# One core, one attention and FP4 feed-forward layer: two accumulators change places, four steps of the hand-written engine orders are moved

## What is computed

```python
y  = layernorm(x)
y1 = LN(y  + causal_attention(y, y, y))        # gains g1, beta1
y2 = LN(y1 + attention(y1, ctx, ctx))          # gains g2, beta2
y3 = LN(y2 + relu(y2 @ w1 + b1) @ w2 + b2)     # 256 -> 1024 -> 256, gains g3, beta3
x1 = x + y3
n  = layernorm(x1)
h  = silu(q(n) @ q(w_gate).T) * (q(n) @ q(w_up).T)   # 256 -> 704
out = x1 + q(h) @ q(w_down).T                        # 704 -> 256
```

## Time and profile before

| what | value |
|---|---|
| time of the profiled execution | 672.63 us |
| its span, first to last instruction | 670.7 us |
| median of the three runs | 672.4 us |
| mean granted TensorE clock | 0.949 |
| TensorE matmul busy | 573.5 us (86%) |
| TensorE weight loads busy | 540.4 us (81%) |
| VectorE busy | 531.6 us (79%) |
| ScalarE busy | 382.1 us (57%) |
| GpSimd busy | 344.4 us (51%) |

### The profile page before, as it was taken

One profiled execution on the slowest core, in us unless ns is written; L12 is line 12 of the kernel. 1 busy time (PEld: TensorE's weight loads), 2 busy tenths in 40 slices (PEclk: granted clock), 3 DMA queues, 4 the chain that ended last, 5 costly groups with the idle time before them and its releaser, 6 DMA issues.

```text
span 670.7 us, 12397 instructions
## 1 busy us (share of the span) xinstructions
PE 573.5 (86%) x3989; PEld 540.4 (81%) x3989; DVE 531.6 (79%) x1305; ACT 382.1 (57%) x779; POOL 344.4 (51%) x444
## 2 busy tenths in 40 slices
PE   2734877999899989999999999998999999988575
PEld 1623776989898989898989889898989898888564
DVE  3965636988887988888888889898879888888763
ACT  3423536666675747475756666665748474756341
POOL 3322235656554755566555655565557555555422
PEclk9575779999999999999999999999999999999986
DMA  7330000101010101000010102010101000000000
GB/s 234 88 98 0 0 33 0 41 1 49 0 56 1 35 15 32 25 23 23 0 55 0 47 0 55 0 47 0 54 1 32 1 24 9 10 9 9 8 17 16
DMA packets 18726, 19.30 MB, mean 29 GB/s; under 512 B 1520, under 2 KB 18176, under 8 KB 18688
## 3 DMA queue, kind: packets, MB, share of 16 engines
q1 hardware_dynamic: 18688, 18.82, 9.4%
HBM read 14.62 MB, written 4.19 MB: 28 GB/s over the span
## 4 chain that ended last, share of the span: by engine, by line
PE 53%; DVE 27%; issue 8%; ACT 6%; POOL 2%; DMA 2%; SPq 1%; DVEq 0%; ACTq 0%; POOLq 0%
PE R L851 4%; PE R L853 4%; PE R L852 4%; PE O L899 3%; PE R L918 3%; PE O L966 3%; PE O L964 3%; PE O L965 3%; PE TR L766 3%; PE R L920 3%; PE R L919 3%; PE R L766 3%; DVE hs L1219 3%; DVE hqT_lo L1252 2%; DVE hT_lo L1246 2%
## 5 line engine op out<-in xcount | busy, mean ns | idle before, releaser
L437 POOL TENSOR_TENSOR rs<-mv,neg_half 128x1 f32<-128x1 f32 (+1 forms) x112 | 68.1, 614 | 43.8 <-DVE mv L1166 41.8
L851 PE MATMUL R<-gu_hi,xqT_hi 128*128 128x352 f32 x256 | 85.5, 334 | 2.3 <-ACT xqT_hi L599 1.1
L918 PE MATMUL R<-y2T_hi,w_hi 128*128 128x256 f32 x256 | 76.7, 300 | 8.0 <-DVE y2T_lo L1302 5.8
L853 PE MATMUL R<-gu_hi,xqT_lo 128*128 128x352 f32 x256 | 82.5, 322 | 0.0
L852 PE MATMUL R<-gu_lo,xqT_hi 128*128 128x352 f32 x256 | 82.5, 322 | 0.0
L443 POOL TENSOR_TENSOR hs<-hh,h_rec 128x704 f32<-128x704 f32 x32 | 44.5, 1392 | 68.5 <-DVE h_rec L1202 68.5
L635 ACT ACTIVATE hqT_hi<-R 128x768 fp32r<-128x768 f32 x32 | 26.0, 812 | 91.3 <-PE R L766 91.3
L964 PE MATMUL O<-w_hi,hT_hi 128*128 128x256 f32 x256 | 74.0, 289 | 0.0
L920 PE MATMUL R<-y2T_hi,w_lo 128*128 128x256 f32 x256 | 72.9, 285 | 0.0
L919 PE MATMUL R<-y2T_lo,w_hi 128*128 128x256 f32 x256 | 72.7, 284 | 0.0
L966 PE MATMUL O<-w_hi,hT_lo 128*128 128x256 f32 x256 | 72.6, 283 | 0.0
(11 more groups left out here) (148 smaller groups left out, 1859.2 us busy)
## 6 DMA issues: line engine op xcount, KB each, us to landing
x_in<-in_x SPq DMA_DIRECT2D x16, 256.0 KB, 2.8
x_res<-in_x SPq DMA_DIRECT2D x16, 256.0 KB, 2.8
out<-x SPq DMA_DIRECT2D x32, 128.0 KB, 1.7
hT<-in_L_xattn_w SPq DMA_DIRECT2D x2, 1024.0 KB, 7.2
ctx_rows<-in_ctx SPq DMA_DIRECT2D x16, 64.0 KB, 2.6
wd_raw<-in_L_ffn_w_down SPq DMA_DIRECT2D x1, 704.0 KB, 11.5
w_raw<-in_L_ffn_w_gate SPq DMA_DIRECT2D x1, 640.0 KB, 5.2
w_raw<-in_L_ffn_w_up SPq DMA_DIRECT2D x1, 640.0 KB, 6.8
```

Of the source, the lines that this page charges most:

```text
L437: pool.tensor_tensor(rs[i][:, t0:t0 + len(ts)], mv[i][:, t0:t0 + len(ts), 1], neg_half[:, 0:len(ts)], ALU.pow).then_inc(ln_rstd[i], 1)
L851: mm(o, xh, gu_hi[:, c, m, cols], start=(c == 0), stop=False)
L853: last = mm(o, xl, gu_hi[:, c, m, cols], start=False, stop=(c == KC - 1))
L918: mm(o, w1_hi[:, c, cols], y2T_hi[:, c, :], start=(c == 0), stop=False)
```

## The change

The same instructions are issued, with the same operands except for the accumulators; they stand in another order on four engines.

- `values` and `down` of tile t now use O[t], so tile 0's values wait for `cross_sum` and tile 1's for `ff_sum`; `ff2` of tile 0 waits for both `down_add`, `cross_values` for the first alone. The second `down_add` moves from behind the products of h to behind `x_max` of tile 1.
- VectorE: the low halves of tile 1's turned h stand ahead of x's block maximum of tile 0 (they stood behind x's reciprocal). The small second piece of `hT_lower` is a function of its own, `hT_stack`. The low half of tile 0's turned h is taken in the slot before, ahead of the second `ff_sum`, and the first two steps of a slot are now the reciprocal and the sum of the self attention. `z3_stats(1)` stands ahead of `x1_sum(0)`; `h_lower` of group 3 moves up to group 2; `cross_max` stands ahead of `h_lift(0)`; the statistics of z2 stand ahead of h's second scale.
- ScalarE: the turned y2 is copied ahead of the first layer norm (`norm_x`); `warm(Exp)` stands ahead of `abs_h(0)`; `norm(2)` stands ahead of `abs_h(1)`; `relu_upper(3)` stands ahead of the second silu.
- GpSimd: `y_rows` of z2 and `context_values` stand at the slot's start, ahead of `unscale_h(1)`; `residual` stands behind `unscale_h(0)`; `power(1)` ahead of `masks`; `power(2)` ahead of `scale_h(1)`.

SyncE's list is unchanged. In it the stores of x2 stand behind a wait for `residual`.

```diff
@@ gpsimd, slot
                 prepare(b, h, "early")
+                if f:
+                    y_rows(b, h, False, 0)
+                    y_rows(b, h, False, 1)
                 if f1:
                     gamma3(b, g, 0)
+                if live(b, h, 0) and h == 0:
...
+                    context_values(b)
                 if q1:
                     unscale_h(b, g, 1)
...
                 if q:
                     unscale_h(b, h, 0)
+                if f:
+                    residual(b, h)
+                prepare(b, h, "late")
+                if a:
+                    power(2, b, h, A, (0, 1))
+                if q:
                     scale_h(b, h, 1)
-                prepare(b, h, "late")
-                if a:
-                    power(2, b, h, A, (0, 1))
@@ scalar, slot
                 if q:
                     silu(b, h, 1, (1,))
+                    warm(b, h, ACT.Exp, 1)
                     abs_h(b, h, 0)
-                    warm(b, h, ACT.Exp, 1)
@@ tensor, values
-                    wait(pe, z3_set, b, h, F + 1, T, T)
-                else:
-                    wait(pe, z2_set, b, h, F, T, T)
+                    wait(pe, z2_set, b, h, F, T, T)
+                else:
+                    wait(pe, z3_set, b, h, F + 1, T, T)
...
-                    last = mm(O[1 - t][:, 0:D + 1], e, y0[:, key, :], start=(i == 0), stop=(i == len(lhs) - 1))
+                    last = mm(O[t][:, 0:D + 1], e, y0[:, key, :], start=(i == 0), stop=(i == len(lhs) - 1))
@@ vector, slot
                 prepare(b, h, "early")
-                if q1:
-                    hT_lower(b, g, 0)
-                if f1:
-                    shift(3, b, g, F, (0,))
                 if a:
                     self_reciprocal(b, h, 0)
                     self_sum(b, h, 0)
                 if q1:
+                    hT_stack(b, g, 0)
+                if f1:
+                    shift(3, b, g, F, (0,))
...
                 if f1:
+                    z3_stats(b, g, 1)
                     x1_sum(b, g, 0)
                     x1_stats(b, g, 0)
+                    aggregate(3, b, g, F, 1)
                     aggregate(4, b, g, F, 0)
-                    z3_stats(b, g, 1)
-                    aggregate(3, b, g, F, 1)
                     x_norm(b, g, 0)
+                if q1:
+                    hT_lower(b, g, 1)
+                    hT_stack(b, g, 1)
+                if f1:
                     x_max(b, g, 0)
+                    shift(3, b, g, F, (1,))
                     x_scale(b, g, 0)
                     x_reciprocal(b, g, 0)
-                    shift(3, b, g, F, (1,))
-                if q1:
-                    hT_lower(b, g, 1)
...
                 if q:
                     h_product(b, h, 1, 1)
+                if a:
+                    cross_max(b, h)
+                if q:
                     h_lift(b, h, 0)
-                if a:
-                    cross_max(b, h)
-                if q:
                     h_drop(b, h, 0)
                     h_max(b, h, 1)
```

More of the change, by code:

```diff
@@ L492, in slot @@
                 prepare(b, h, "early")
+                if f:
+                    y_rows(b, h, False, 0)
+                    y_rows(b, h, False, 1)
                 if f1:
                     gamma3(b, g, 0)
+                if live(b, h, 0) and h == 0:
+                    if isinstance(b, int) and b == 0:
+                        pool.wait_ge(beta1_in, 16)
+                    context_values(b)
                 if q1:
@@ L509, in slot @@
                     unscale_x(b, g, 1)
+                if a:
+                    power(1, b, h, A, (0, 1))
                 if live(b, h, 0):
                     masks(b, h)
-                if a:
[L513 to L519, removed]
                 prepare(b, h, "mid")
@@ L699, in slot @@
                                    ACT.Copy).then_inc(y2T_hi_set, 1)
+                if front:
+                    norm_x(b, h)
                 if q1:
@@ L727, in slot @@
                     xT_upper(b, h, 1)
+                if f:
+                    relu_upper(b, h, (3,))
+                if q:
                     silu(b, h, 0, (1,))
@@ L755, in slot @@
                     norm(2, b, h, A, 1, 1, z2[:, 1, :], z2[:, 1, :])
+                if q:
+                    abs_h(b, h, 1)
                 prepare(b, h, "end")
@@ L955, in ff2 @@
                     if fs[0] == 0:
-                        wait(pe, x2_set, b, h, Q + 1, T, 1)
+                        wait(pe, x2_set, b, h, Q + 1, T, T)
                 else:
@@ L976, in cross_values @@
                     wait_batch(pe, ctx_lo_set, b, 1, 1)
-                wait(pe, x2_set, b, h, Q + 1, T, T)
+                wait(pe, x2_set, b, h, Q + 1, T, 1)
                 for t in range(T):
@@ L1306, in self_reciprocal @@
                 wait(dve, pv_done, b, h, A, T, t + 1)
-                v.reciprocal(rsum1[:, t:t + 1], O[1 - t][:, D:D + 1]).then_inc(rsum1_set, 1)
+                v.reciprocal(rsum1[:, t:t + 1], O[t][:, D:D + 1]).then_inc(rsum1_set, 1)
             def self_sum(b, h, t):
@@ L1381, in slot @@
                     x1_stats(b, g, 1)
-                    aggregate(4, b, g, F, 1)
                 if q1:
                     down_add(b, g, 0)
+                if f1:
+                    aggregate(4, b, g, F, 1)
                 if f:
@@ L1389, in slot @@
                     x_max(b, g, 1)
+                if q1:
+                    down_add(b, g, 1)
+                if f1:
                     x_scale(b, g, 1)
@@ L1420, in slot @@
                     h_product(b, h, 1, 0)
-                if f:
-                    h_lower(b, h, (3,))
-                if q1:
-                    down_add(b, g, 1)
                 if front:
@@ L1431, in slot @@
                     h_product(b, h, 1, 1)
-                    h_lift(b, h, 0)
                 if a:
@@ L1435, in slot @@
                 if q:
+                    h_lift(b, h, 0)
                     h_drop(b, h, 0)
@@ L1454, in slot @@
                     aggregate(2, b, h, A, 1)
+                if q:
+                    h_scale(b, h, 1)
+                    h_reciprocal(b, h, 1)
                 if f:
                     z3_stats(b, h, 0)
+                if a:
+                    shift(2, b, h, A, (0, 1))
+                if q:
+                    hT_lower(b, h, 0)
+                if f:
+                    ff_sum(b, h, 1)
                     aggregate(3, b, h, F, 0)
-                    ff_sum(b, h, 1)
                 if front:
                     shift(0, b, h + 1, 0, (0, 1))
-                if a:
-                    shift(2, b, h, A, (0, 1))
                 prepare(b, h, "end")
```

24 lines of the change are left out of this document (8 added, 16 removed).

## The result

The changed kernel takes **696.5 us** (median of four runs, 692.5 to 697.1), the kernel before, run beside it, 671.6: a ratio of 1.0345, 95% interval 1.0316 to 1.0375. The forecast was 682.0 us and the range ended at 688. The direction was right, the size was not. The profiled execution took 696.46 us with a span of 694.5, so 23.8 us of span have to be found.

A forecast was written before the change was run, and what follows sets the result against it. TensorE sets the pace and VectorE decides how long it stands. Even slots +7.0, odd slots -1.8, head -0.8 and tail +5.3 make +9.7 us on 672.4: 682 us, forecast range 676 to 686, wider range 671 to 688.

The forecast's parts named there:

- the drain: Slots 16 to 19, where no new rows come in; the prediction's tail, without other slots' work, was put at +5.3 us.
- the head: Slots 2 and 3: turned y2 copied ahead of x's layer norm, saving 0.8 us, bounds 0 and -1.6.
- Part 2: ScalarE's Exp table load ahead of h's magnitudes: costs 0.6 us into an even slot, 0.4 into an odd one.
- Part 1: Exchanged accumulators and the slot's head: wins 0.7 and 0.5 us into an even slot, 0.3 into an odd one.
- Part 3: VectorE takes tile 1's turned h ahead of x's maximum: +1.6 us into an even slot, -0.3 into an odd one.
- Part 4: The rest: h's low halves taken off GpSimd's long products, about 1.6 us of VectorE; residual moved later; no effect.
- E: End of hT_upper(1) on ScalarE, the reference time in a slot; 358.29 us in slot 10 of the kernel before.
- the mark: Start of gate and up on TensorE, from which each slot's interval is measured.
- Rival 4: ScalarE stands behind each table load, 1.28 us before h's magnitudes in 16 slots: 703 us, chance 0.01.
- rival 3: Even slots also pay 0.5 us for quantised h late behind context_values, odd ones gain nothing: 688 us, chance 0.08.
- Rivals 1 and 2: Waits go and nothing replaces them, 667 us, chance 0.15; or steady slots come out even, 674 us, chance 0.10.

The follow-up runs named there:

- e3: Changed kernel with Part 2 and Part 3 both undone in every slot: 674.9 us, ratio 1.0023 to the kernel before.
- f4: e3 with GpSimd's list put back in the order of the kernel before: 689.2 us, ratio 1.0259.
- f3: The kernel before with unused matmuls put ahead of TensorE's waits in slots 16 to 19: 671.9 us, ratio 0.9991.
- e4: Changed kernel with Part 2 and Part 3 undone only in the draining slots 16 to 19: 682.9 us, ratio 1.0143.
- f1: Changed kernel with unused matmuls in slots 16 to 19, slot 16's group ahead of tile 0's down, where TensorE doesn't wait: 690.7 us, ratio 1.0267.
- g1: Changed kernel with unused matmuls ahead of TensorE's waits in slots 16 to 19, slot 16's group ahead of tile 1's down: 687.9 us, ratio 1.0215.
- g2: Changed kernel with Part 2 undone, Part 3 kept only in odd slots up to 15, unused matmuls in the drain: 668.3 us, ratio 0.9924.
- e2: Changed kernel with Part 2 alone undone in every slot: 681.7 us, ratio 1.0126.
- g4: e3 with GpSimd's row steps back in the old order, z2's root kept ahead of tile 1's quantised h: 679.7 us, ratio 1.0094.
- g3: g2 with VectorE's two-element step nm of z2 moved behind the low half of tile 0's turned h: 663.6 us, ratio 0.9864.
- e1: Changed kernel with Part 3 alone undone in every slot: 685.0 us, ratio 1.0169.

## Why the prediction was right and wrong

**What failed.** The forecast was +9.7 us and the span grew by 23.8. The largest part of the 14.1 us between them is a term that the sum didn't have, TensorE's clock in the drain: 6.8 us. The odd intervals come next, forecast at -1.8 us together and measured at +1.5, then slot 17, 2.0 us, and less than 1 us each from the even intervals, from slot 16 and from the head.

**The steady even slot** was forecast at +1.0 us and measured +1.1, yet not by my terms. Part 2 was +0.6, measured +0.66. Parts 1 and 3 were -1.2 and +1.6, measured -0.38 (with part 4) and +0.82. I had taken each wait by itself. Of the 0.52 us ahead of the values 0.39 remain in e3, for tile 1. And what the slot's head wins TensorE then stands at the scores, for the small piece of the turned h: 0.96 us in e3 against 0.31 in the kernel before. With part 3 that wait is 0.31 again, which I had credited to odd slots alone, and the delay behind it comes on top. From E to the mark it is 7.80 us in the kernel before (358.29 to 366.09), 8.43 in e3 (427.52 to 435.95) and 9.26 in the changed kernel (434.53 to 443.79): 0.83 for part 3, and not 1.6. That the two errors of 0.8 us cancel is in part this shared wait and in part luck. Part 3's own mechanism held: x's scale at E + 2.2, `e_diag` in front of ff1's third group (0.64 us, forecast 1.5), the mark 1.5 us later against E than before the change.

**The steady odd slot** was forecast at -0.3 and measured 0.0. Part 2 cost 0.44 to 0.49 (forecast 0.4) and part 3 won 0.43 to 0.48 (0.3). Part 1's 0.3 us and y2's 0.1 didn't come: tile 1's values wait 0.93 us. I left out that `ff_sum(1)` itself moves behind `nm` and tile 0's turned h, and that `nm` runs into GpSimd's product.

**Part 4** was said to bring nothing. On top of e3 it is worth 2.6 us a pair of slots. The other moves without it (f4, with parts 2 and 3 undone as well) make the kernel slower: 73.75 us a pair, against 71.58. Its cost is absent from the sum because I weighed the new list of GpSimd against VectorE's old one. `h_scale(1)` had moved behind z2's statistics, so the root had to move as well.

**The head** was forecast at -0.8 us and came out at -0.1, but single executions don't settle this. The mark of slot 3 stands at 117.00 us in the kernel before and at 115.76 in f3, which has the same code up to there; in the changed kernel, e4, f1 and g1 it stands between 116.54 and 117.31. ff1 of slot 2 starts at 73.39 us, 0.84 earlier than in the earlier trace rows, and in these other runs at 73.94 (f3) and 73.51 to 74.03. So the gain of 0.8 us isn't shown, and what takes it back, if it is there, stays open.

**The drain** was forecast at +6.3 (1.0, 1.35, 2.8, 1.1 for its four stretches, rounded) and measured +15.5. With the clock held (g1 against the kernel before, its last two stretches from f3) the stretches differ by 1.8, 3.4, 2.5 and 1.0: 8.7 us. Slots 18 and 19 are as forecast, slot 16 cost 0.8 us more than its 1.0, and slot 17 2 us more than the 1.35 I gave it. Of slot 17's 3.4 us, 1.4 stay with parts 2 and 3 undone (34.23 us in g2 against 32.80); which of the other moves makes them stays open. Of the 8.7, parts 2 and 3 make 6.9 (133.12 - 126.25 in g2, which has them undone there and the clock held). **The other 6.8 us are TensorE's clock**: it costs 8.1 us here and 1.3 before. This term is missing in my sum. I had every duration of the drain from rows of the kernel before, whose clock was 1.00 up to slot 17, and put longer waits behind them without asking what longer waits do to the matmuls that follow. It also goes with e2's 14.9 us for 8: in its drain the same matmuls keep TensorE busy 6.2 us less than in the changed kernel.

**The rivals.** Rival 4 (ScalarE stands behind each table load) is out: magnitudes 2.15 us behind the last silu, the load 1.28, and 0.02 us behind it the warm word. The Trainium skill's drain (ScalarE: Activation LUTs, What ACT_TABLE_LOAD costs) doesn't show in these rows. The cause that rival 3 names is out: an even interval takes 34.69 us with `context_values` moved (e3) and 34.68 with it and the other row steps where they stood (g4). Its other half, odd slots that gain nothing, came true for the reasons above. Rivals 1 and 2 needed a pair of 71.6 us or less; it is 72.7.

## What to carry to other kernels

Price a new wait of TensorE twice where little other work surrounds it: once as time, and once as the matmuls that follow at half the clock. The draining slots are the place, and a run with unused matmuls ahead of the waits tells the two apart. Two moves that touch the same wait don't add, so follow the next wait after each one. Look at each short VectorE step for what GpSimd does at that moment: an order that suits one engine's list can be ruined by the other's.

## What the runs showed of the hardware

A VectorE step of 128x2 elements took 1.34 us, in every steady slot, where it fell beside a GpSimd product of 128x704; it started 0.06 us behind that product and ended with it (388.36 + 1.39 = 389.75). The first row is GpSimd's, the second VectorE's, slot 10 of the changed kernel:

```profile
388.36 1.39 POOL L443 TENSOR_TENSOR hs<-hh,h_rec 128x704 f32<-128x704 f32 x1
388.42 1.34 DVE L1174 SCALAR_TENSOR_TENSOR nm<-mv,rs 128x2 f32<-128x2 f32 x1
```

The same step takes 0.16 us in f4, where it doesn't meet that product; in the kernel before, two such steps together take 0.22. In g3 it starts later, takes 0.67 us and again ends with the product (377.23 + 0.67 = 377.90; 376.49 + 1.39 = 377.88). So a step that is short by itself can lose as much as one of 128x512 elements does in the earlier trace rows. The Trainium skill (GPSIMD Engine Reference, Specifications) says that GpSimd contends for SBUF with VectorE instructions that have two SBUF inputs. The step has two, `mv` and `rs`, and the trace agrees.

In the drain of the changed kernel the granted clock first fell after TensorE had stood 2.49 us. At the same place it fell after 2.49 (f1) and 2.48 us (e2), and didn't after 1.47 (the kernel before), 1.79 (e4), 1.87 (e1) and 1.89 us (e3). The length of the last wait isn't all, though: ahead of the turn of z2 in slot 17 TensorE stands 1.82 us in the changed kernel and 1.82 us in e4, and the clock falls to 0.50 in the first and stays at 1.00 in the second. Ten groups of 11 to 32 unused matmuls held it at 1.00 up to the end. Whether fewer would do wasn't tried, nor was the first 100 us, in parts of which the clock is low in every run here.
